# W1's units quantised first and p1 of the first two tiles put ahead of batch 3's values, in an attention and MXINT8 feed-forward kernel

## The chip, the cores and the metric

The kernel runs on one core of a Trainium2 chip. The metric is the device time of one execution in microseconds. Three runs of the kernel before took 282.99, 283.56 and 286.78 us, a median of 283.56.

## What is computed

For four batches of 512 tokens with 512 features and a context of 512 x 256:

```python
query = einsum('bnc,dc->bnd', ctx, Wq) + bq          # D = 128
key   = einsum('bnc,dc->bnd', ctx, Wk) + bk
attention = softmax(einsum('bnd,bmd->bnm', query, key))
x = x + einsum('bln,bmn->blm', layernorm(x), attention)

v = bf16(layernorm(x)); residual = v
h = bf16((v - mean(v)) * rsqrt(var(v) + 1e-5) * ln_w + ln_b)
h = bf16(mx_quant(h) @ mx_quant(W1).T + b1)          # 512 -> 2048
h = bf16(gelu_tanh(h))
h = bf16(mx_quant(h) @ mx_quant(W2).T + b2)          # 2048 -> 512
x = x + bf16(residual + h)
```

`mx_quant` rounds each block of 32 along the contraction to 8-bit integers with a shared power-of-two scale, from the block's largest absolute value.

## The kernel before

The program is written by hand, one instruction stream per engine, with semaphores between them. The order of each stream is the order of its code.

**Attention** goes batch by batch (`batch` on PE and ACT, `front` and `back` on VectorE, DVE). PE makes `energies` (L649), ACT the exponentials, DVE the low halves of p and x (`p_low`, `x_low`), SyncE (SP) transposes them by DMA (`xT` at L237, `pT` at L244), and PE makes `values` of the four 128-token tiles (L661, then L664, which adds x). ACT takes each out of PSUM in `x_plus` (L482) with its sum, takes the squares in `x1_square` (L490), POOL makes the row factors (`factors_x1`), and ACT writes the normalised rows v in `v_out` (L497) and their sums in `v_sums` (L505, L508). POOL's `factors_v` makes the factors of the second layer norm, and DVE applies it, a tile at a time, with `times_w` and `plus_b` (L961, L966), into `hq`. The block quantisation of a batch's `hq` is `h1_amax` to `h1_mult`, and gives `h1q`.

**Weights.** W1 and W2 come in four units each, [128, 2048] floats. There are two slots of the staging buffer `wst`, W1's and W2's. A unit goes through `w_amax` (L764), power, scale, inverse, `w_over` (L807), `w_clip` and `w_mult` (L817) on DVE, in steps placed in `front` and `back`, and then through a DMA transpose on SP (`w1_transpose`, `w2_transpose`). Unit u of W1 is finished in batch u's `back`, unit u of W2 in `front` of batch u+1, the last one after batch 3.

**Feed-forward**: 16 tiles of 128 tokens; tile i is (m, k) with i = 2m + k. For each one: SP transposes `h1q` (`h1_transpose`, L274, into `h1T`, which lies over cxT); PE makes p1 (`product1`: four bias matmuls L707 and 16 matmuls L712, into four PSUM banks); ACT takes the two halves out and applies GELU (`y_out`, L558 and L562, into `gs`, over phl); DVE quantises in `slot(m, k, tail)`; SP transposes the result (`h2_transpose`, L287); PE makes p2 (`product2`, 16 matmuls L722); ACT's `z_out` (L571), POOL's or DVE's two adds and SP's store end the tile. On PE p1 runs three tiles ahead of p2. Buffers are doubled. `ys` lies over the first slot of `wst`, `h2u` over `wquant`.

A DVE slot of tile i holds the clip of tile i-1, the block maximum (L764) of tile i, the last multiply (L871) of tile i-1, scale and inverse, and the multiply by the inverse (L861) of tile i. `tail` is other work put between them, as layer-norm steps of a coming batch. In `tail_parts(b)` parts 0 to 3 are the layer norm of batch b's four tiles, part 4 the block maximum and scales of h1, part 5 its three large operations.

PE's order before the steady loop is: values 0, p1(0), values 1, p1(1), values 2, values 3, p1(2), then steps.

Of the kernel before, what the change touches and what calls it, by code (L numbers as in the profile page):

```python
# [29 lines left out]
def xattn_ffn_kernel(nc, x, ctx_in, wq, bq, wk, bk, ln_w, ln_b, w1, b1, w2, b2, out):  # L30
# [25 lines left out]
    with ExitStack() as stack:  # L56
# [155 lines left out]

        @block.sync
        def _(sp):
# [37 lines left out]
            def w1_transpose(u):
                wait_alone(sp, w_step[W1], W_STEPS * (u + 1), sp_gate)
                sp.dma_start_transpose(
                    w1T[:, bass.ds(4 * u, 4), :, :].rearrange("p r k f -> p (r k) f"), wquant[:, W1, :])\
                    .then_inc(w1T_rdy, 16)

            def w2_transpose(u):
                wait_alone(sp, w_step[W2], W_STEPS * (u + 1), sp_gate)
                sp.dma_start_transpose(w2T[:, :, bass.ds(P * u, P)], wquant[:, W2, :]).then_inc(w2T_rdy, 16)  # L260
# [895 lines left out]
```

## Time and profile before

| | |
|---|---|
| runs, us | 282.99, 283.56, 286.78; median 283.56 |
| profiled execution, us | 283.25 |
| its span, us | 281.4 |
| busy of the span | DVE 89%, PE 81%, ACT 60%, POOL 25% |
| granted TensorE clock, mean | 0.927 of full speed |
| chain that ended last, by engine | DVE 45%, PE 25%, ACT 11%, DMA 8% |

The span runs from the first to the last instruction of the profiled execution, in microseconds from its start. A busy share is an average over the span. In the timelines a row is one instruction, or several of a kind merged (x4); the number in brackets is how long the engine stood idle before it, and who ended that. PE rows can overlap by a few tenths, since matmuls are pipelined and their ends are modelled.

### The profile page before, as it was taken

How to read it: one execution, taken by the hardware profiler on the slowest of the kernel's cores; microseconds unless marked ns; L12 is line 12 of the kernel's file. 1: busy time of each engine (PE TensorE's matmuls, PEld its weight loads, DVE VectorE, ACT ScalarE, POOL GpSimd, SP SyncE). 2: the span in 40 equal slices, each digit the busy share in tenths (PEclk: the TensorE clock that was granted, in tenths of full speed). 3: DMA queues.
4: the chain of work that ended last, by engine and by line, in shares of the span. 5: the costliest groups of instructions: out<-in, count | busy, mean ns of one | idle time of the engine just before them, and what ended most of it. 6: DMA issues, size and time to landing. Idle time of an engine off the chain costs nothing.

```text
span 281.4 us, 3244 instructions
## 1 busy us (share of the span) xinstructions
PE 228.7 (81%) x937; PEld 99.4 (35%) x946; DVE 249.2 (89%) x377; ACT 169.4 (60%) x287; POOL 69.0 (25%) x96
## 2 busy tenths in 40 slices
PE   7748739996998059651699969799999989999993
PEld 7314313443433024210244433344444434444431
DVE  2388999999988899999979999599999999877992
ACT  2337216628995447845987599966566554665610
POOL 1058100022004500053060050413333233333400
PEclk9985886999999759975899999999999999999999
DMA  4963999999997952939623045635355555555683
GB/s 157 378 250 89 227 279 201 297 238 194 263 257 190 221 91 38 222 59 194 124 52 62 0 93 70 119 62 123 88 122 129 130 130 131 130 130 114 139 178 130
DMA packets 103077, 42.92 MB, mean 152 GB/s; under 512 B 93844, under 2 KB 96152, under 8 KB 102552
## 3 DMA queue, kind: packets, MB, share of 16 engines
q1 hardware_dynamic: 100224, 35.93, 58.6%
q10 hardware_dynamic: 2360, 6.83, 7.7%
q8 instruction: 5, 0.08, 0.1%
q0 software_dynamic: 480, 0.02, 0.1%
q14 instruction: 8, 0.07, 0.1%
HBM read 15.48 MB, written 4.19 MB: 70 GB/s over the span
## 4 chain that ended last, share of the span: by engine, by line
DVE 45%; PE 25%; ACT 11%; DMA 8%; issue 5%; POOL 4%; SPq 2%; ACTq 0%; DVEq 0%; POOLq 0%
DVE amax L764 12%; PE ps L722 9%; PE ps L712 8%; PE ps L661 4%; DVE w_int L807 4%; DMA xhl<-pf 3%; DVE hq L966 3%; DVE stats L918 3%; DMA wst<-in_L_ffn_W 3%; DVE vw L961 3%; DVE pf L871 3%; DVE phl L942 2%; DVE wquant L861 2%; POOL rs L350 2%; DVE xhl L954 2%
## 5 line engine op out<-in xcount | busy, mean ns | idle before, releaser
L661 PE MATMUL ps<-pT,xT 128*128 128x512 f16 x192 | 49.7, 414 | 14.1 <-DMA pT<-phl 11.0
L722 PE MATMUL ps<-w2T,xhl 128*128 128x512 bf16 x247 | 56.5, 379 | 2.9 <-DMA xhl<-pf 2.4
L712 PE MATMUL ps<-w1T,cxT 128*128 128x512 bf16 x256 | 58.0, 380 | 0.0
L558 ACT ACTIVATE wst<-ps 128x1024 bf16<-128x1024 f32 x32 | 32.3, 1019 | 27.9 <-PE ps L712 27.9
L764 DVE TENSOR_REDUCE amax<-phl 128x64 f32<-128x2048 bf16 x16 | 36.5, 2280 | 6.9 <-ACT phl L562 6.9
L649 PE MATMUL ps<-qkT 128*128 128x512 f32 x32 | 19.5, 715 | 22.7 <-ACT pf L457 18.8
L661 PEld LDWEIGHTS ps<-pT,xT 128*128 128x128 f16 x192 | 19.9, 106 | 48.0 <-issue 31.8
L722 PEld LDWEIGHTS ps<-w2T,xhl 128*128 128x128 bf16 x256 | 24.6, 98 | 33.2 <-DMA xhl<-pf 4.2
L712 PEld LDWEIGHTS ps<-w1T,cxT 128*128 128x128 bf16 x256 | 23.7, 98 | 32.6 <-issue 6.2
L562 ACT ACTIVATE phl<-wst 128x2048 bf16<-128x2048 bf16 x16 | 30.6, 1910 | 1.3
L423 POOL TENSOR_TENSOR wst<-wst,vs 128x512 bf16<-128x512 bf16 x12 | 14.8, 1233 | 55.5 <-DVE wquant L866 55.5
L764 DVE TENSOR_REDUCE amax<-wst 128x64 f32<-128x2048 f32 x8 | 18.2, 2270 | 6.1 <-DMA wst<-in_L_ffn_W 6.1
L457 ACT ACTIVATE pf<-ps,nmax 128x512 f32<-128x512 f32 x16 | 10.9, 681 | 19.8 <-DVE nmax L928 19.7
L571 ACT ACTIVATE wst<-ps 128x512 bf16<-128x512 f32 x16 | 9.5, 595 | 16.2 <-PE ps L722 15.8
L861 DVE TENSOR_TENSOR wquant<-phl,mxi 128x2048 int16<-128x2048 bf16 x15 | 18.3, 1223 | 0.3
L641 PE MATMUL ps<-cxT,wqkT 128*128 128x512 f32 x32 | 16.5, 663 | 2.5 <-ACT cxT L447 2.5
L807 DVE TENSOR_TENSOR w_int<-wst,mxi 128x2048 int16<-128x2048 f32 x8 | 18.3, 2285 | 0.0
L871 DVE TENSOR_TENSOR pf<-wquant,mxs 128x2048 bf16<-128x2048 int16 x15 | 18.2, 1216 | 0.0
L649 PEld LDWEIGHTS ps<-qkT 128*128 128x128 f32 x32 | 5.9, 212 | 32.3 <-ACT pf L457 21.8
L355 POOL TENSOR_SCALAR rs<-mv 128x4 f32<-128x4 f32 x4 | 0.9, 227 | 65.6 <-DVE mv L923 65.6
L664 PE MATMUL ps<-xs,ident_x 128*128 128x512 f32 x32 | 16.3, 592 | 0.0
L482 ACT ACTIVATE xs<-ps 128x512 f32<-128x512 f32 x16 | 9.4, 586 | 9.7 <-PE ps L664 9.7
(79 smaller groups left out, 357.4 us busy)
## 6 DMA issues: line engine op xcount, KB each, us to landing
wst<-in_L_ffn_W ACTq DMA_DIRECT2D x6, 1024.0 KB, 6.1
xs<-in_x SPq DMA_DIRECT2D x4, 1024.0 KB, 8.4
out_x<-wst SPq DMA_DIRECT2D x16, 256.0 KB, 2.8
cx<-in_ctx SPq DMA_DIRECT2D x4, 512.0 KB, 5.8
wst<-in_L_ffn_W SPq DMA_DIRECT2D x2, 1024.0 KB, 10.3
xhl<-pf SPq DMA_TRANSPOSE x17, 4.3
xT<-xhl SPq DMA_TRANSPOSE x16, 4.6
pT<-phl SPq DMA_TRANSPOSE x16, 3.3
```

Of the source, the lines that this page charges most:

```text
L558: act.activation(ys[:, k, 1024 * g:1024 * g + 1024], ps_y[:, 2 * g:2 * g + 2, :], ACT.Copy)\
L562: act.activation(gs[:, k, :], ys[:, k, :], ACT.Gelu_apprx_tanh).then_inc(g_rdy, 1)
L641: last = pe.matmul(ps_qk[:, a, :], wqkT[:, a, c, :], cxT[:, c, :], start=(c == 0), stop=(c == CT - 1))
L649: pe.matmul(ps_e[:, t % 2, :], qkT[:, 0, P * t:P * t + P], qkT[:, 1, :], start=True, stop=True).then_inc(e_ps, 1)
L661: pe.matmul(ps_pv[:, t % 2, :], xT[:, t, NT * a + n, :], pT[:, :, NT * c + n, :], start=(s == 0), stop=False)
L664: pe.matmul(ps_pv[:, t % 2, :], ident_x[:, :], xs[:, LT * b + t, :], start=False, stop=True).then_inc(pv_ps, 1)
L712: last = pe.matmul(ps_y[:, c, :], h1T[:, k, t, :], w1T[:, 4 * c:4 * c + 4, t, :], start=False, stop=(t == KT - 1))
L722: last = pe.matmul(ps_z[:, k, :], h2T[:, k, t, :], w2T[:, t, :], start=False, stop=(t == FT - 1))
L764: dve.tensor_reduce(amax[:, a, :], by_block, AX_X, ALU.max, apply_absolute_value=True)\
L807: dve.tensor_tensor(blocks(w_int[:, :]), blocks(wst[:, a, :]), inverse, ALU.mult)\
L861: dve.tensor_tensor(pairs(h2u[:, k, :]), pairs(gs[:, k, :]), per_block(mxi[:, k, :, :]), ALU.mult).then_inc(h2_step[k], 1)
L871: dve.tensor_tensor(pairs(h2q[:, k, :]), pairs(h2u[:, k, :]), per_block(mxs[:, k, :, :]), ALU.mult).then_inc(h2_step[k], 1)
```

## The change

Weights: the two slots of `wst` are named EVEN and ODD and hold units of both matrices in a new order, given by the table UNITS. EVEN holds W1's units 0, 2, 3 and W2's 2; ODD holds W1's 1 and W2's 0, 1, 3. W1's last unit is so transposed in batch 2. SP's loop over batches 2 and 3 is written out.

First products: SP transposes `h1q` of tiles 0 and 1 ahead of batch 3's last pT. PE makes p1(0) and p1(1) ahead of batch 3's four values. ACT's `y_out` is split into `y_evict` and `gelu`; y(0) and y(1) are evicted among the `v_sums` of batch 2, and their GELUs come behind these.

Layer norms: DVE does batch 2's in the slots of tiles 1 to 4 and batch 3's in those of tiles 5 to 8. ACT's `x1_square` and `v_sums` of batch 3 are spread between evictions, and POOL's `factors_v(3)` comes after tile 0's adds.

```diff
-        W1, W2, H1 = range(3)
+        EVEN, ODD, H1 = range(3)
+        UNITS = (("w1", 0), ("w1", 2), ("w1", 3), ("w2", 2)), (("w1", 1), ("w2", 0), ("w2", 1), ("w2", 3))
...
+        def load_unit(eng, slot, u):
+            kind, n = UNITS[slot][u]
+            if kind == "w1":
+                return eng.dma_start(wst[:, slot, :].rearrange("p (r k) -> p r k", r=4), w1_t[n])
+            return eng.dma_start(wst[:, slot, :], w2_t[n])
...
                 for t in range(NT):
+                    if b == B - 1 and t == NT - 1:
+                        sp.wait_ge(h1_step, H_STEPS)
+                        sp.wait_ge(qk_ps, 2 * B)
+                        h1_transpose(0, 0)
+                        h1_transpose(0, 1)
                     wait_alone(sp, p_lo, b * NT + (t + 1), sp_gate)
...
-                w1_transpose(b)
+                if b > 0:
+                    transpose_unit(ODD, b - 1).then_inc(oddT_rdy, 16)
+                transpose_unit(EVEN, b).then_inc(evenT_rdy, 16)
...
-            with sp.Fori(2, B) as b:
-                front(b)
+            front(2)
...
-            sp.wait_ge(h1_step, H_STEPS)
-            sp.wait_ge(qk_ps, 2 * B)
-            h1_transpose(0, 0)
-            h1_transpose(0, 1)
-            w2_transpose(B - 1)
+            front(B - 1)
+            transpose_unit(ODD, B - 1).then_inc(oddT_rdy, 16)
...
-            factors_v(B - 1)
...
             for i in range(T - ON_DVE):
+                if i == 1:
+                    factors_v(B - 1)
                 add_residual(i)
                 add_x(i)
...
             for t in range(LT):
                 v_out(B - 2, t)
+            act.wait_ge(w_step[EVEN], W_STEPS * (B - 1) + 5)
+            y_evict(0, 0)
             v_sums(B - 2, 0)
             v_sums(B - 2, 1)
+            y_evict(0, 1)
             v_sums(B - 2, 2)
             v_sums(B - 2, 3)
             for t in range(NT):
                 act.wait_ge(pT_rdy[t], 16 * B)
-            for k in range(2):
-                x_plus(B - 1, k)
-                y_out(0, k)
-            x_plus(B - 1, 2)
-            x_plus(B - 1, 3)
-            for t in range(LT):
-                x1_square(B - 1, t)
+            gelu(0, 0)
+            x_plus(B - 1, 0)
+            gelu(0, 1)
+            for t in range(1, LT):
+                x_plus(B - 1, t)
+            x1_square(B - 1, 0)
+            x1_square(B - 1, 1)
             y_out(1, 0)
+            x1_square(B - 1, 2)
+            x1_square(B - 1, 3)
+            y_out(1, 1)
             for t in range(LT):
                 v_out(B - 1, t)
-            step(0, 0)
-            for t in range(LT):
-                v_sums(B - 1, t)
-            step(0, 1)
-            with act.Fori(1, T // 2 - 2) as m:
+            z_out(0, 0)
+            y_out(2, 0)
+            v_sums(B - 1, 0)
+            z_out(0, 1)
+            v_sums(B - 1, 1)
+            y_out(2, 1)
+            v_sums(B - 1, 2)
+            v_sums(B - 1, 3)
+            z_out(1, 0)
+            step(1, 1)
+            with act.Fori(2, T // 2 - 2) as m:
...
-            values(B - 1, 0)
...
-            pe.wait_ge(w1T_rdy, 16 * B)
+            pe.wait_ge(evenT_rdy, 16 * 3)
+            pe.wait_ge(oddT_rdy, 16)
+            pe.wait_ge(qk_sb, 2 * B)
+            product1(0, 0)
+            product1(0, 1)
             pe.wait_ge(p_exp, T)
-            for k in range(2):
-                if k > 0:
-                    values(B - 1, k)
-                product1(0, k)
-            values(B - 1, 2)
-            values(B - 1, 3)
+            for t in range(LT):
+                values(B - 1, t)
             product1(1, 0)
...
-            parts = tail_parts(B - 2)
-            for part in parts[:LT]:
-                for part_step in part:
-                    part_step()
-            dve.wait_ge(w1T_rdy, 16 * B)
-            slot(0, 0, parts[LT], True)
-            dve.wait_ge(w2T_rdy, 16 * B)
-            slot(0, 1, parts[LT + 1])
-            slot(1, 0, [])
-            parts = tail_parts(B - 1)
-            parts = [[], parts[0], parts[1] + parts[2]] + parts[3:]
-            for i in range(3, 3 + len(parts)):
-                slot(i // 2, i % 2, parts[i - 3])
+            p2, p3 = tail_parts(B - 2), tail_parts(B - 1)
+            dve.wait_ge(evenT_rdy, 16 * B)
+            slot(0, 0, [], True)
+            dve.wait_ge(oddT_rdy, 16 * B)
+            slot(0, 1, p2[0] + p2[1])
+            slot(1, 0, p2[2] + p2[3])
+            slot(1, 1, p2[LT])
+            slot(2, 0, p2[LT + 1])
+            slot(2, 1, p3[0])
+            slot(3, 0, p3[1] + p3[2])
+            slot(3, 1, p3[3] + p3[LT])
+            slot(4, 0, p3[LT + 1])
```

The names W1, W2, `ld_w1`, `w1T_rdy`, `load_w1` and so on become EVEN, ODD, `ld_even`, `evenT_rdy`, `load_even` throughout.

**PE, around the first products.** L661 and L664 are values, L707 and L712 are p1 (in the change L686, L689, L732, L737). Before, from the values of batch 3's first tile:

```order
L661 MATMUL ps<-pT,xT 128x512 x12
L664 MATMUL ps<-xs,ident_x 128x512
L707 MATMUL ps<-b1row,ones 128x512 x4
L712 MATMUL ps<-w1T,cxT 128x512 x16
L661 MATMUL ps<-pT,xT 128x512 x12
L664 MATMUL ps<-xs,ident_x 128x512
L707 MATMUL ps<-b1row,ones 128x512 x4
L712 MATMUL ps<-w1T,cxT 128x512 x16
L661 MATMUL ps<-pT,xT 128x512 x12
L664 MATMUL ps<-xs,ident_x 128x512
L661 MATMUL ps<-pT,xT 128x512 x12
L664 MATMUL ps<-xs,ident_x 128x512
```

and in the change, from the same place:

```order
L732 MATMUL ps<-b1row,ones 128x512 x4
L737 MATMUL ps<-w1T,cxT 128x512 x16
L732 MATMUL ps<-b1row,ones 128x512 x4
L737 MATMUL ps<-w1T,cxT 128x512 x16
L686 MATMUL ps<-pT,xT 128x512 x12
L689 MATMUL ps<-xs,ident_x 128x512
L686 MATMUL ps<-pT,xT 128x512 x12
L689 MATMUL ps<-xs,ident_x 128x512
L686 MATMUL ps<-pT,xT 128x512 x12
L689 MATMUL ps<-xs,ident_x 128x512
L686 MATMUL ps<-pT,xT 128x512 x12
L689 MATMUL ps<-xs,ident_x 128x512
```

Both p1 went ahead of the first values.

**ACT, from the end of batch 2's v_sums to the second GELU.** A pair of `squares` and `vs,sums<-vs` is one v_sums, `wst<-ps` x2 the eviction of a y, `phl<-wst` a GELU, `xs,sums<-ps` an x_plus. Before:

```order
L505 ACTIVATE squares,sums<-vs 128x512
L508 ACTIVATE vs,sums<-vs 128x512
L482 ACTIVATE xs,sums<-ps 128x512
L558 ACTIVATE wst<-ps 128x1024 x2
L562 ACT_TABLE_LOAD
L562 ACTIVATE phl<-wst 128x2048
L482 ACTIVATE xs,sums<-ps 128x512
L558 ACTIVATE wst<-ps 128x1024 x2
L562 ACTIVATE phl<-wst 128x2048
```

and in the change:

```order
L565 ACTIVATE wst<-ps 128x1024 x2
L512 ACTIVATE squares,sums<-vs 128x512
L515 ACTIVATE vs,sums<-vs 128x512
L512 ACTIVATE squares,sums<-vs 128x512
L515 ACTIVATE vs,sums<-vs 128x512
L572 ACT_TABLE_LOAD
L572 ACTIVATE phl<-wst 128x2048
L489 ACTIVATE xs,sums<-ps 128x512
L572 ACTIVATE phl<-wst 128x2048
```

The eviction of y(1) stands ahead of the last two v_sums, that of y(0) two v_sums further ahead, right behind v_out. The first x_plus went behind the first GELU.

**DVE, from the last weight unit to tile 1's maximum.** `w_int` and `wquant<-w_int` are the last unit, a pair of `vw` and `hq<-vw` is the layer norm of one tile, `amax<-phl` a tile's block maximum. Before, with the first of four layer-norm pairs:

```order
L807 TENSOR_TENSOR w_int<-wst,mxi 128x2048
L812 TENSOR_SCALAR w_int<-w_int 128x2048
L817 TENSOR_TENSOR wquant<-w_int,mxs 128x2048
L961 SCALAR_TENSOR_TENSOR vw<-vs,mean,lnw 128x512
L966 SCALAR_TENSOR_TENSOR hq<-vw,rs,lnb 128x512
```

and in the change:

```order
L831 TENSOR_TENSOR w_int<-wst,mxi 128x2048
L836 TENSOR_SCALAR w_int<-w_int 128x2048
L841 TENSOR_TENSOR wquant<-w_int,mxs 128x2048
L788 TENSOR_REDUCE amax<-phl 128x64
L796 TENSOR_SCALAR pow<-amax 128x64
L802 TENSOR_SCALAR mxs<-pow 128x128
L807 TENSOR_SCALAR mxi<-mxs 128x128
L885 TENSOR_TENSOR wquant<-phl,mxi 128x2048
L890 TENSOR_SCALAR wquant<-wquant 128x2048
L788 TENSOR_REDUCE amax<-phl 128x64
```

Nothing is left between the last unit and tile 0's maximum; the four pairs stand in the slots of tiles 1 and 2.

## Rows read from the trace of the kernel before

**Rows 1.** Page, part 1: busy us, share of the span, instructions.

```profile
PE 228.7 (81%) x937; PEld 99.4 (35%) x946; DVE 249.2 (89%) x377; ACT 169.4 (60%) x287; POOL 69.0 (25%) x96
```

**Rows 2.** DVE timeline, 144 to 227: start us, us, engine line op out<-in, [idle before].

```profile
146.45 0.75 DVE L961 SCALAR_TENSOR_TENSOR vw<-vs,mean,lnw 128x512 f32<-128x512 bf16 x1 [1.55 <-POOL rs L350]
...
152.25 2.28 DVE L764 TENSOR_REDUCE amax<-phl 128x64 f32<-128x2048 bf16 x1
...
168.08 2.28 DVE L764 TENSOR_REDUCE amax<-phl 128x64 f32<-128x2048 bf16 x1
...
173.99 2.28 DVE L764 TENSOR_REDUCE amax<-phl 128x64 f32<-128x2048 bf16 x1
...
182.82 2.29 DVE L764 TENSOR_REDUCE amax<-phl 128x64 f32<-128x2048 bf16 x1 [2.84 <-ACT phl L562]
...
189.94 2.28 DVE L764 TENSOR_REDUCE amax<-phl 128x64 f32<-128x2048 bf16 x1
...
198.53 2.28 DVE L764 TENSOR_REDUCE amax<-phl 128x64 f32<-128x2048 bf16 x1
...
222.99 2.28 DVE L764 TENSOR_REDUCE amax<-phl 128x64 f32<-128x2048 bf16 x1
...
225.58 1.21 DVE L871 TENSOR_TENSOR pf<-wquant,mxs 128x2048 bf16<-128x2048 int16 x1
```

**Rows 3.** PE timeline, 132 to 250.

```profile
132.47 4.29 PE L661 MATMUL ps<-pT,xT 128*128 128x512 f16 x12 [9.24 <-DMA pT<-phl]
...
139.79 0.40 PE L707 MATMUL ps<-b1row,ones 3*128 3x512 bf16 x4 [2.17 <-DMA cxT<-h1q]
140.12 3.63 PE L712 MATMUL ps<-w1T,cxT 128*128 128x512 bf16 x16
...
150.92 2.75 PE L661 MATMUL ps<-pT,xT 128*128 128x512 f16 x12
...
154.37 2.75 PE L661 MATMUL ps<-pT,xT 128*128 128x512 f16 x12
...
168.14 3.40 PE L722 MATMUL ps<-w2T,xhl 128*128 128x512 bf16 x15
...
231.38 3.63 PE L722 MATMUL ps<-w2T,xhl 128*128 128x512 bf16 x16 [0.96 <-DMA xhl<-pf]
...
246.48 3.62 PE L722 MATMUL ps<-w2T,xhl 128*128 128x512 bf16 x16
```

**Rows 4.** Windows, PE's wait before batch 3's values; 0.63 is PE's granted clock.

```profile
123.00:132.50 9.50, 0.26 (x2) 0.06 (x2) 9.39 (x15) 3.62 (x10) 5.79 (x9) 0.63 0.87 158
```

**Rows 5.** ACT timeline, 132 to 170.

```profile
132.64 2.93 ACT L497 ACTIVATE vs<-xs,off,rs 128x512 bf16<-128x512 f32 x4 [3.00 <-POOL off L370]
135.47 0.61 ACT L505 ACTIVATE squares<-vs 128x512 bf16<-128x512 bf16 x1
...
140.94 0.58 ACT L482 ACTIVATE xs<-ps 128x512 f32<-128x512 f32 x1
...
142.06 1.02 ACT L558 ACTIVATE wst<-ps 128x1024 bf16<-128x1024 f32 x1 [0.46 <-PE ps L712]
...
144.83 1.28 ACT L562 ACT_TABLE_LOAD   x1
146.12 1.91 ACT L562 ACTIVATE phl<-wst 128x2048 bf16<-128x2048 bf16 x1
...
158.02 0.60 ACT L482 ACTIVATE xs<-ps 128x512 f32<-128x512 f32 x1 [2.76 <-PE ps L664]
...
161.89 1.91 ACT L558 ACTIVATE wst<-ps 128x1024 bf16<-128x1024 f32 x2
...
166.40 2.93 ACT L497 ACTIVATE vs<-xs,off,rs 128x512 bf16<-128x512 f32 x4 [0.66 <-POOL off L370]
```

**Rows 6.** SP's queue, 124 to 140: issue start, us over all.

```profile
124.76 5.36 SPq L244 DMA_TRANSPOSE pT<-phl  x4
...
137.00 2.76 SPq L274 DMA_TRANSPOSE cxT<-h1q  x2
```

More of the change, by code:

```diff
@@ L247, in front, with transpose_unit @@
                     load_x(later)
-                if not isinstance(b, int) or b > 0:
-                    w2_transpose(b - 1)
-                w1_transpose(b)
[L252 to L260, printed above, removed]
+                if b > 0:
+                    transpose_unit(ODD, b - 1).then_inc(oddT_rdy, 16)
+                transpose_unit(EVEN, b).then_inc(evenT_rdy, 16)
+            def transpose_unit(slot, u):
+                kind, n = UNITS[slot][u]
+                wait_alone(sp, w_step[slot], W_STEPS * (u + 1), sp_gate)
+                if kind == "w1":
+                    return sp.dma_start_transpose(
+                        w1T[:, 4 * n:4 * n + 4, :, :].rearrange("p r k f -> p (r k) f"), wquant[:, slot, :])
+                return sp.dma_start_transpose(w2T[:, :, P * n:P * n + P], wquant[:, slot, :])
             load_ctx(1)
@@ L523, in batch @@
                     if t == 2 and b is not None:
-                        load_w2(front)
+                        load_odd(front)
                     if v is not None and t > 0:
@@ L531, in batch @@
                 if not isinstance(front, int) or front + 1 < B:
-                    load_w1(front + 1)
+                    load_even(front + 1)
                 if b is not None:
@@ L559, in y_out, with gelu @@
                        .then_inc(y_sb, 1)
+            def gelu(m, k):
+                i = 2 * m + k
                 act.wait_ge(y_sb, 2 * i + 2)
@@ L562, in y_out @@
                 act.activation(gs[:, k, :], ys[:, k, :], ACT.Gelu_apprx_tanh).then_inc(g_rdy, 1)
+            def y_out(m, k):
+                y_evict(m, k)
+                gelu(m, k)
             def z_out(m, k):
@@ L571, in z_out, with step @@
                 act.activation(zs[:, k, :], ps_z[:, k, :], ACT.Copy).then_inc(z_sb, 1)
+            def step(m, k):
+                if not isinstance(m, int) or 2 * m + k + 3 < T:
+                    y_out(*tile(m, k, 3))
+                z_out(m, k)
             for t in range(LT):
                 v_out(B - 2, t)
+            act.wait_ge(w_step[EVEN], W_STEPS * (B - 1) + 5)
+            y_evict(0, 0)
             v_sums(B - 2, 0)
             v_sums(B - 2, 1)
+            y_evict(0, 1)
             v_sums(B - 2, 2)
@@ L814, in w_mult @@
             def w_mult(a, u):
-                wait(dve, (w1T_rdy, w2T_rdy)[a], 16 * u)
+                wait(dve, (evenT_rdy, oddT_rdy)[a], 16 * u)
                 dve.wait_ge(w_step[a], W_STEPS * u + 6)
@@ L1047, in back @@
                         plus_b(tail, t)
-                w_clip(W1, w1)
-                w_mult(W1, w1)
+                w_clip(EVEN, w1)
+                w_mult(EVEN, w1)
             def tail_parts(b):
@@ L1060, in _ @@
             split3(b2_step, b2f, b2p)
-            w_amax(W1, 0)
-            w_power(W1, 0)
-            w_scale(W1, 0)
-            w_inverse(W1, 0)
+            w_amax(EVEN, 0)
+            w_power(EVEN, 0)
+            w_scale(EVEN, 0)
+            w_inverse(EVEN, 0)
             x_stats(0)
```

63 lines of the change are left out of this document (30 added, 33 removed).

## The prediction, made before the changed kernel ran

> **What bounds the kernel now.** I read the page's busy shares first: VectorE (DVE) 89%, TensorE (PE) 81% [rows 1]. An average over stages with different limits decides nothing, so I took the timelines of DVE, PE, ScalarE (ACT) and SyncE (SP) from the last batch of attention to the feed-forward tiles. Three things are to be seen.
>
> First, DVE works without a gap until the last weight unit is done. It then waits 1.55 us (until 146.45, so from 144.90) for the row factors of batch 2's layer norm, does that layer norm, and starts tile 0's block maximum at 152.25 [rows 2]. From there it goes from slot to slot, one slot per tile and one block maximum at the start of each. Its only other wait before tile 9 is 2.84 us, on ACT's GELU of tile 4 [rows 2]. DVE is thus idle 1.55 + 2.84 = 4.39 us between 144.90 and tile 9's maximum at 222.99.
>
> Second, PE's second product of tile 8 starts at 231.38, after a wait of 0.96 us for the transposed values [rows 3]. These come from DVE's multiply at 225.58 in slot 9 [rows 2]. That start stands 231.38 - 222.99 = 8.39 us behind the maximum of tile 9. After it every DVE slot is shorter than PE's 7.55 us a tile, (246.48 - 231.38) / 2 (a slot with nothing added takes 173.99 - 168.08 = 5.91 us [rows 2, 3]), and PE sets the end. So the end moves one for one with the later of two things: DVE's arrival at tile 9, and PE's own work before tile 8's second product.
>
> Third, before the feed-forward PE stands idle 9.24 us (from about 123.2), then 2.17 us more, then makes p1 of tiles 0 and 1 between the values; two sets of values without a gap are 154.37 - 150.92 = 3.45 us apart [rows 3]. The granted clock of 123.0 to 132.5 is 0.63 on average [rows 4], a mix of 2.4 and 1.2 GHz. The twelve matmuls after the wait take 4.29 us where the same twelve take 2.75 later [rows 3]. A start after that idle therefore costs about 1.5 us.
>
> **The slots of the weights.** The same eight units are loaded, quantised and transposed, by the same DVE forms. Only which matrix a slot holds changes. The SP loop becomes straight code, without its branches. I cost both at nothing. Their cover is DVE's gapless work: without it the loop could give or take at most about one issue of SP, 1.34 us [rows 6], since it runs through twice.
>
> **SP's order.** The four pT transposes of batch 3 are issued from 124.76 in 5.36 us, 1.34 each [rows 6]. In the change h1T of tiles 0 and 1 go in ahead of the fourth, at about 128.8, 1.34 us each. The fourth pT goes at about 131.5 instead of 128.8. Its readers, the values of batch 3, are now behind p1 on PE and start past 142, so this is hidden. Odd unit 2 is transposed at about 132.8, and DVE wants that slot back for unit 3 about 143: covered by some 10 us. If that cover went, DVE's arrival would move with it.
>
> **PE and ACT up to the first GELU.** This is the term that counts.
> - h1T(0) lands about 2.8 us after its issue (137.00 to 139.79 [rows 3, 6]): PE starts p1(0) at about 131.7. At full clock p1 takes 140.12 + 3.63 - 139.79 = 3.96 us. With 1.5 more for the clock it ends at about 137.2, its first half at 131.7 + 2.27 + 1.5 = 135.5 (139.79 to the eviction at 142.06 [rows 3, 5]).
> - ACT ends its four v_out at 132.64 + 2.93 = 135.57 [rows 5]. It evicts the halves of y(0) at 135.6 and 137.3, 1.02 each: done 138.3. PE's p1(1) waits for that and runs 138.4 to 142.4.
> - Two of four v_sums, which take 140.94 - 135.47 = 5.47 together, 2.74 for two [rows 5]: 141.1. Halves of y(1) at 141.1 and 142.4: done 143.4. Two more v_sums: 146.1.
> - Table load and GELU(0), 1.28 and 1.91 [rows 5]: **149.3**. Before, GELU(0) ended at 148.03, but DVE had layer-norm work until 152.25. Now it has none and waits from 144.90 to 149.3: 4.4 us of idle in place of 1.55.
>
> The table load stands directly in front of the GELU: 144.83 and 146.12 [rows 5], 1.29 us from start to start. The Trainium skill (ScalarE: Activation LUTs, What ACT_TABLE_LOAD costs) puts about 1.38 us of drain on top of each switch. By that rule the GELU would end 1.4 us later and the total below would be +2.4; the row shows no such gap, so the row is used.
>
> **The second wait.** ACT now does x_plus(0), then GELU(1), then x_plus(1). So PE makes the values of tile 2 from 150.0 (3.45 each), those of tile 3 to 156.9, and p1(2) to 160.8. The fourth pT has long landed by then. ACT, from x_plus(3) at 157.0: in the old order the step from 158.02 to 161.89 held x_plus, POOL's mean and four squares [rows 5]. With two squares (0.71 each) in place of four it is 2.45: 159.45. Second half of y(2) out at 161.8, GELU(2) at 163.7. DVE: slot 0 without its tail takes 4.8 us (5.91 less the 1.2 us multiply, which slot 0 has not), slot 1 now holds two tiles of layer norm, as slot 5 did (198.53 - 189.94 = 8.59 [rows 2]). So it is ready for tile 2's maximum at 149.35 + 4.8 + 8.59 = 162.75 and waits **0.95**.
>
> The later tiles have cover. Two squares (165.1), y(3) out (167.1), GELU(3) 169.0; DVE comes for it at 163.8 + 8.59 = 172.4. POOL's factors for v_out took 4.5 us behind the squares (161.89 to 166.40), so v_out of batch 3 ends at 165.1 + 4.5 + 2.93 = 172.5, z(0) at 173.1, y(4) is out at 175.0 and GELU(4) ends at 177.0; DVE comes at 172.4 + 5.91 or later. So the 2.84 us wait goes. PE's second product of tile 0 starts at about 165.9 instead of 168.14, since p1(3) starts when y(2) is out at 161.8 and takes 4.1 with its bias. By slot 3 it waits for DVE's results on every tile.
>
> **The layer norms moved.** Four pairs of operations of batch 2 go from ahead of slot 0 into slots 1 and 2, 5.8 us (146.45 to 152.25). The block work of h1 goes from slots 0 and 1 into 3 and 4, and batch 3's loses its free slot. All of it is still done before tile 9: DVE's sum of work between 144.90 and 222.99 is unchanged, which is why its idle time alone decides. Batch 3's factors on POOL now stand between tiles 0 and 1 of the residual adds. Their sums end on ACT at about 186.9 (from 177.0: a v_sums 1.4, z(1) 0.6, a v_sums 1.4, y(5) and its GELU 3.8, two v_sums 2.7), and batch 2's factors took 146.45 - 140.94 = 5.5 us behind theirs [rows 2, 5]: 192.4. DVE asks at about 193.3: nothing, with 1 us to spare.
>
> **Sum.** 4.40 + 0.95 - 4.39 = +0.96 us on DVE's way to tile 9, and so on the end. The profiled execution took 283.25 us (span 281.4), 0.31 below the median 283.56. So 284.2 on its scale, **284.5** as a median. Bounds of the term: GELU(0) can't end before 135.57 + 3.82 + 5.47 + 3.19 = 148.05 (four halves, four v_sums, load and GELU in one row), total -0.3. At the other end it ends at 155.5 (second rival), total +7.2. I take 149.3, since each wait in it is read from a neighbouring row.
>
> **Rivals.**
> 1. PE is the bound: its lead of 168.14 - 165.9 = 2.2 us reaches the end. For it: the chain behind tile 8 is PE's, and the front of the change is PE work. Against: PE's wait of 0.96 on DVE's output, and the slots' sum. The time is 283.56 - 2.2 = 281.3. At most all 4.39 us of DVE's idle goes, 279.2. Chance 0.20.
> 2. The clock stays down, the case that is slower. PE starts p1(0) after 8.5 us of idle, and p1(0) and p1(1) are parted by waits for ACT. If both run wholly at 1.2 GHz, p1(0) ends at 139.6 and is out at 140.6, p1(1) runs to 148.6 and is out at 149.6, two v_sums 152.3, GELU(0) 155.5. That is 6.2 later and +7.2 in all: 290.8. It decides from the point where p1(0)'s second half is still at half clock. Against: twelve matmuls were enough in the old order, after a longer idle, and a 2.17 us gap behind them cost nothing [rows 3]. The Trainium skill (TensorE: Matmul & The Clock Gate, Part 1) has idle gaps between bursts throttling the clock again each time; the 2.17 us gap here did not. Chance 0.07.
> 3. The change doesn't do what it says: the layer norm moved to slot 5 finds no factors, since they stand on POOL behind tile 0's adds and on ACT behind y(5), and DVE stops there. Price 1 to 2 us on top of the forecast, 286. Chance 0.10.
>
> **How the numbers follow.** Forecast 0.63, with its own range 283.2 to 286.0 (GELU(0) from 148.05 to 150.8). The range of 281.0 to 287.0 takes in most of the first rival and the third, and leaves out the second and the first's far end. Two per cent (5.7 us) is about what a measurement of this kernel tells from no change. The first rival can't reach that, since only 4.39 us of idle are there to win: faster 0.03 for what I have not seen. Slower 0.06, nearly all the second rival. Within 0.91.
>
> **What would show it.** Right: DVE idle of about 4.4 us before tile 0's maximum, about 1 before tile 2's, none at tile 4; p1(0) from about 131.7 and its first matmuls slow; PE's second product of tile 0 about 2 us sooner and of tile 8 not sooner, with PE waiting for DMA at most tiles from 2 to 8. Wrong: tile 0's maximum before 148.5, or tile 9's before 222, or a DVE wait on POOL in slot 5.

## The result, and the profile after

| | before | changed |
|---|---|---|
| median of 18 runs each, us | 283.79 | 285.44 |
| lowest and highest | 281.44, 287.64 | 283.21, 286.68 |
| profiled execution, us | 283.25 | 285.30 |
| its span, us | 281.4 | 283.5 |

The ratio of the changed kernel to the one before is 1.0069, with a 95% interval of 1.0042 to 1.0095: slower by 1.2 to 2.7 us, well inside two per cent. The forecast was 284.5 us, +0.96. The sign was right. The size was about half of what came, and the profile shows where the other half arose. Some executions of each kernel come out 1 to 2% longer than its fastest; the ratios leave them out, the medians don't, and the profiled executions of "v_sums(2) first" and of the first "GELU(0) first" below are of that kind.

The page's busy shares. DVE is 1.0 us busier than in [rows 1]. PE's 2.0 us more is mostly nine matmul records that the trace before lacks (x937 for x946), about 0.2 us each:

```profile
PE 230.7 (81%) x946; PEld 99.3 (35%) x946; DVE 250.2 (88%) x377; ACT 169.1 (60%) x287; POOL 66.1 (23%) x96
```

DVE's timeline, the rows that answer to [rows 2] (last weight multiply, then block maxima of tiles 0, 1, 2, 3, 4, 5, 6 and 9):

```profile
143.28 1.23 DVE L841 TENSOR_TENSOR wquant<-w_int,mxs 128x2048 bf16<-128x2048 int16 x1
149.32 2.29 DVE L788 TENSOR_REDUCE amax<-phl 128x64 f32<-128x2048 bf16 x1 [4.82 <-ACT phl L572]
...
154.31 2.28 DVE L788 TENSOR_REDUCE amax<-phl 128x64 f32<-128x2048 bf16 x1
...
163.92 2.29 DVE L788 TENSOR_REDUCE amax<-phl 128x64 f32<-128x2048 bf16 x1 [1.09 <-ACT phl L572]
...
172.36 2.28 DVE L788 TENSOR_REDUCE amax<-phl 128x64 f32<-128x2048 bf16 x1
...
180.69 2.28 DVE L788 TENSOR_REDUCE amax<-phl 128x64 f32<-128x2048 bf16 x1
...
189.41 2.28 DVE L788 TENSOR_REDUCE amax<-phl 128x64 f32<-128x2048 bf16 x1
...
197.68 2.28 DVE L788 TENSOR_REDUCE amax<-phl 128x64 f32<-128x2048 bf16 x1
...
225.06 2.28 DVE L788 TENSOR_REDUCE amax<-phl 128x64 f32<-128x2048 bf16 x1
```

Tile 9's maximum is 2.07 us later than the 222.99 of [rows 2], and the span is 2.1 longer. In its terms: the weights are done 0.40 earlier (144.50 for 144.90), idle time is 4.82 + 1.09 = 5.91 in place of 4.39 (+1.52), and the time DVE is not waiting is 80.56 - 5.91 = 74.65 in place of 78.09 - 4.39 = 73.70 (+0.95). The last was forecast as unchanged. It lies in the slot of tile 5, 197.68 - 189.41 = 8.27 us with one tile of layer norm, where the slot of tile 4 before took 189.94 - 182.82 = 7.12 with the same work [rows 2].

DVE in that slot, and then POOL at the same time (both timelines, same columns):

```profile
191.72 0.46 DVE L796 TENSOR_SCALAR pow<-amax 128x64 uint32<-128x64 uint32 x1
192.10 1.21 DVE L895 TENSOR_TENSOR pf<-wquant,mxs 128x2048 bf16<-128x2048 int16 x1
193.24 1.64 DVE L985 SCALAR_TENSOR_TENSOR vw<-vs,mean,lnw 128x512 f32<-128x512 bf16 x1
```

```profile
187.23 0.49 POOL L382 TENSOR_SCALAR mean<-sums 128x4 f32<-128x4 f32 x1 [3.92 <-ACT vs L515]
...
189.97 1.04 POOL L356 TENSOR_TENSOR rs<-rs,half 128x4 f32<-128x4 f32 x1
190.97 1.16 POOL L428 TENSOR_TENSOR wst<-wst,vs 128x512 bf16<-128x512 bf16 x1
192.21 2.12 POOL L434 TENSOR_TENSOR wst<-xs,wst 128x512 f32<-128x512 f32 x1
```

Batch 3's factors run from 187.23 to 191.01. So the adds of tile 1 begin 1.6 us behind the block maximum of 189.41. In the kernel before they began 0.23 us behind one (190.17 and 189.94). The second stands from 192.21 to 194.33 beside DVE's two-input operations: it takes 2.12 us, and the layer-norm operation 1.64 where its neighbours take 0.75. The ends fit two engines taking turns. POOL starts 0.11 us behind DVE's `pf` and ends 1.02 us behind that operation's end (193.31); `vw` starts while POOL holds on and ends 0.55 behind POOL's end. The Trainium skill (SBUF — State Buffer, SBUF: two separate sides) states such a rule: a DVE operation with two SBUF inputs and a GpSimd operation that reads SBUF exclude each other, whoever starts first holds the port pair, and "the other fully blocks". The trace agrees. It agrees also with what the rule leaves free: a maximum, with one input, beside the same adds costs neither anything (2.28 and 1.16, below). I had not weighed that rule.

PE, the rows that answer to [rows 3], and its granted clock by stretches (window, its length, PE busy, clock, DMA share, GB/s):

```profile
130.99 0.62 PE L732 MATMUL ps<-b1row,ones 3*128 3x512 bf16 x4 [8.13 <-DMA cxT<-h1q]
131.54 5.51 PE L737 MATMUL ps<-w1T,cxT 128*128 128x512 bf16 x16
138.26 0.40 PE L732 MATMUL ps<-b1row,ones 3*128 3x512 bf16 x4 [1.21 <-ACT wst L565]
138.59 3.63 PE L737 MATMUL ps<-w1T,cxT 128*128 128x512 bf16 x16
...
166.07 3.62 PE L747 MATMUL ps<-w2T,xhl 128*128 128x512 bf16 x16
...
233.43 3.63 PE L747 MATMUL ps<-w2T,xhl 128*128 128x512 bf16 x16 [0.97 <-DMA xhl<-pf]
```

```profile
131.00:135.00 4.00, 4.00 (x13) 0.50 0.89 168
135.00:136.00 1.00, 1.00 (x5) 0.81 1.12 196
136.00:137.00 1.00, 1.00 (x5) 1.00 1.12 213
```

Sixteen matmuls behind the 8.13 us wait take 5.51 for 3.63, at 1.2 GHz up to about 135. The second product of tile 0 is 2.07 us sooner than in [rows 3], that of tile 8 2.05 later: PE's lead is used up in waits.

ACT, the rows that answer to [rows 5]:

```profile
135.23 1.02 ACT L565 ACTIVATE wst<-ps 128x1024 bf16<-128x1024 f32 x1
137.09 1.02 ACT L565 ACTIVATE wst<-ps 128x1024 bf16<-128x1024 f32 x1 [0.83 <-PE ps L737]
...
142.25 1.02 ACT L565 ACTIVATE wst<-ps 128x1024 bf16<-128x1024 f32 x1 [0.50 <-PE ps L737]
...
146.02 1.28 ACT L572 ACT_TABLE_LOAD   x1
147.31 1.91 ACT L572 ACTIVATE phl<-wst 128x2048 bf16<-128x2048 bf16 x1
```

GELU(0) ends at 149.22. From the end of `v_out` (135.18) to the end of GELU(0) ACT has 14.04 us, and waits for PE in them 0.83 and 0.50 us. The rest is both evictions, four `v_sums` and the GELU: what DVE waits for is mainly ACT's order.

### The profile page after: what moved, and what is told of

It is laid out like the page before. It is cut to its first block, busy times and chain, and to the rows that moved or that the text cites. A ratio compares the mean times of both kernels' runs of the same rounds, so it can differ in the third digit from the quotient of the medians.

```text
span 283.5 us, 3197 instructions
## 1 busy us (share of the span) xinstructions
PE 230.7 (81%) x946; PEld 99.3 (35%) x946; DVE 250.2 (88%) x377; ACT 169.1 (60%) x287; POOL 66.1 (23%) x96
## 4 chain that ended last, share of the span: by engine, by line
DVE 48%; PE 26%; ACT 8%; DMA 8%; issue 5%; SPq 3%; POOL 2%; ACTq 0%; DVEq 0%; POOLq 0%
DVE amax L788 13%; PE ps L737 9%; PE ps L747 9%; DVE w_int L831 4%; PE ps L686 4%; DVE pf L895 3%; DMA xhl<-pf 3%; DVE stats L942 3%; DVE wquant L885 3%; DMA wst<-in_L_ffn_W 3%; DVE vw L985 3%; DVE hq L990 2%; DVE phl L966 2%; SPq L257 2%; DVE wquant L890 2%
## 5 line engine op out<-in xcount | busy, mean ns | idle before, releaser
L747 PE MATMUL ps<-w2T,xhl 128*128 128x512 bf16 x256 | 58.0, 379 | 6.2 <-DMA xhl<-pf 6.2
L737 PE MATMUL ps<-w1T,cxT 128*128 128x512 bf16 x256 | 59.9, 388 | 0.0
L686 PE MATMUL ps<-pT,xT 128*128 128x512 f16 x192 | 48.4, 406 | 5.6 <-ACT xs L489 4.5
L737 PEld LDWEIGHTS ps<-w1T,cxT 128*128 128x128 bf16 x256 | 24.2, 100 | 34.2 <-issue 8.9
L686 PEld LDWEIGHTS ps<-pT,xT 128*128 128x128 f16 x192 | 19.5, 103 | 38.8 <-issue 22.1
L732 PE MATMUL ps<-b1row,ones 3*128 3x512 bf16 x64 | 9.2, 395 | 9.3 <-DMA cxT<-h1q 8.1
L689 PE MATMUL ps<-xs,ident_x 128*128 128x512 f32 x32 | 16.3, 592 | 0.0
```

What stands on the lines that cost most here:

```text
L686: pe.matmul(ps_pv[:, t % 2, :], xT[:, t, NT * a + n, :], pT[:, :, NT * c + n, :], start=(s == 0), stop=False)
L689: pe.matmul(ps_pv[:, t % 2, :], ident_x[:, :], xs[:, LT * b + t, :], start=False, stop=True).then_inc(pv_ps, 1)
L737: last = pe.matmul(ps_y[:, c, :], h1T[:, k, t, :], w1T[:, 4 * c:4 * c + 4, t, :], start=False, stop=(t == KT - 1))
L747: last = pe.matmul(ps_z[:, k, :], h2T[:, k, t, :], w2T[:, t, :], start=False, stop=(t == FT - 1))
```

## Experiments

"Way" is the time from the start of DVE's last weight multiply (143.67 before, 143.28 after) to tile 9's maximum. It takes out the stages ahead: between profiled executions that last multiply starts anywhere from 141.34 to 144.90. It does not take out when ACT gets to GELU(0), so the way from tile 0's maximum to tile 9's is given too where that matters. Each ratio is to executions of the kernel before taken together with it (medians 283.37 to 283.88 us). The changed kernel ran 18 times, "LN2 back in front" 4, "the same again" and "changed, factors behind" 6, "the same, factors behind" 12, the others 10.

| kernel | median, us | ratio, interval | way, us |
|---|---|---|---|
| before | 283.79 | 1 | 79.32 |
| changed | 285.44 | 1.0069, 1.0042 to 1.0095 | 81.78 |
| units only | 281.61 | 0.9914, 0.9866 to 0.9961 | 77.78 |
| GELU(0) first | 280.39 | 0.9870, 0.9831 to 0.9910 | 77.64 |
| the same again | 280.71 | 0.9886, 0.9841 to 0.9932 | 77.88 |
| the same, factors behind | 281.45 | 0.9851, 0.9805 to 0.9897 | 78.24 |
| v_sums(3) early | 284.21 | 0.9998, 0.9951 to 1.0045 | 79.66 |
| v_sums(2) first | 284.01 | 1.0014, 0.9975 to 1.0054 | 80.71 |
| warm PE, 26 | 286.42 | 1.0080, 1.0038 to 1.0122 | 82.07 |
| warm PE, 36 | 286.08 | 1.0089, 1.0046 to 1.0132 | 82.34 |
| changed, factors behind | 286.71 | 1.0106, 1.0057 to 1.0154 | 82.03 |
| PE late | 286.50 | 1.0107, 1.0076 to 1.0137 | 82.37 |
| LN2 back in front | 288.45 | 1.0151, 1.0071 to 1.0232 | 84.63 |

The order by way is nearly the order by ratio.

**Batch 2's layer norm back ahead of slot 0**, all else as in the change:

```diff
+            for part in p2[:LT]: ...   # the four tiles
             dve.wait_ge(evenT_rdy, 16 * B)
-            slot(0, 0, [], True)
...
-            slot(0, 1, p2[0] + p2[1])
-            slot(1, 0, p2[2] + p2[3])
-            slot(1, 1, p2[LT])
-            slot(2, 0, p2[LT + 1])
+            slot(0, 0, p2[LT], True)
...
+            slot(0, 1, p2[LT + 1])
+            slot(1, 0, [])
+            slot(1, 1, [])
+            slot(2, 0, [])
```

> The changed kernel with batch 2's layer norm back ahead of slot 0 on DVE, its h1 block work back in slots 0 and 1, slots 2 to 4 without added work. Theory (DVE's idle time before tile 9 decides): POOL's factors of batch 2 end at about 148.4, so DVE waits there from 144.5, 3.9 us, and then no more for GELU(0) or GELU(2): 3.9 us of idle in place of 5.9. Tile 9's maximum at about 223.1 instead of 225.06, the end 2.0 us sooner than in the changed kernel, about level with before (ratio to before 0.998 to 1.003). Rival (PE's own chain decides): PE's order is untouched, so the end stays within 0.5 us of the changed kernel. Rival (the added cost is only POOL's contention in slot 5): also no change, since slot 5 is untouched.

It was far worse: 1.0151 of before, where 0.998 to 1.003 was expected. DVE's waits and what followed the last:

```profile
148.33 0.75 DVE L985 SCALAR_TENSOR_TENSOR vw<-vs,mean,lnw 128x512 f32<-128x512 bf16 x1 [3.77 <-POOL rs L356]
...
189.42 2.29 DVE L788 TENSOR_REDUCE amax<-phl 128x64 f32<-128x2048 bf16 x1 [1.47 <-ACT phl L572]
...
195.20 1.64 DVE L985 SCALAR_TENSOR_TENSOR vw<-vs,mean,lnw 128x512 f32<-128x512 bf16 x1 [2.13 <-POOL rs L356]
196.76 1.17 DVE L802 TENSOR_SCALAR mxs<-pow 128x128 bf16<-128x128 f32 x1
```

Layer norm first waits for the factors, since ACT now makes the v_sums behind two evictions: 3.77 for the 1.55 of before. And empty slots 2 to 4 bring DVE to tile 5 before its GELU and before batch 3's factors. That is 7.37 us of idle against 4.39 before and 5.91 in the changed kernel, with a collision in slot 5 (11.17 us for 8.27, 2.13 of it the wait). Behind ACT's new order the layer norm stands better behind slot 0. The forecast had the first wait right (3.9) and missed the two in slot 5.

**Batch 3's v_sums ahead of y(5)** on ACT:

```diff
             v_sums(B - 1, 1)
-            y_out(2, 1)
             v_sums(B - 1, 2)
             v_sums(B - 1, 3)
+            y_out(2, 1)
```

> The changed kernel with ACT's last two v_sums of batch 3 ahead of y(5) instead of behind it. Theory (POOL's add of tile 1 fell out of tile 5's block maximum since the factors of batch 3 came late, and held up DVE's layer-norm operation, 1.64 us in place of 0.75): the factors end before 189, POOL's adds of tile 1 run beside tile 5's maximum at 189.4, the layer-norm operation in slot 5 takes 0.75 again, slot 5 is 7.1 us in place of 8.27, and the end comes about 1.0 us sooner than in the changed kernel. Rival (slot 5 is long for another reason): slot 5 stays at 8.3 and the end stays. GELU(5) comes about 2.5 us later, at 186.5, still ahead of DVE.

From tile 0's to tile 9's maximum it took 74.74 us, 75.74 in the changed kernel: 1.00 less, as expected. (Its way is 2.12 less, but 1.13 of that is a shorter wait before tile 0, 3.69 for 4.82, which stands ahead of the edit.) DVE in slot 5, then POOL:

```profile
189.80 2.28 DVE L788 TENSOR_REDUCE amax<-phl 128x64 f32<-128x2048 bf16 x1
...
193.53 0.74 DVE L985 SCALAR_TENSOR_TENSOR vw<-vs,mean,lnw 128x512 f32<-128x512 bf16 x1
```

```profile
190.03 1.16 POOL L428 TENSOR_TENSOR wst<-wst,vs 128x512 bf16<-128x512 bf16 x1
191.27 1.16 POOL L434 TENSOR_TENSOR wst<-xs,wst 128x512 f32<-128x512 f32 x1
```

The factors are done just in time, at 190.06. The adds run beside the maximum, the second 0.35 us beyond it, and neither they nor the layer-norm operation are stretched. Slot 5 took 7.28 us for 8.27, with its tile of layer norm still in it. The median is 1.2 us lower, by the ratios 2.0. This shows the second half of the loss.

**PE kept busy ahead of p1(0)**, so that it might start at 2.4 GHz; and the same with 36 small matmuls:

```diff
             pe.wait_ge(c_ones, 1)
+            pe.wait_ge(x1_rdy, (B - 1) * LT)
+            keep_busy(26)
             pe.wait_ge(row_b1, 16 * 3 * LT)
```

> The changed kernel with 26 small matmuls on PE between batch 2's last values and p1(0), which fill its 8 us of idle; their result is not used. Theory (a start at 1.2 GHz costs p1(0) 1.6 to 2 us, and that reaches DVE through the evictions): p1(0)'s 16 matmuls take 3.6 us in place of 5.5, y(0) is out 1.3 to 1.7 us sooner, and GELU(0) and DVE's first maximum come 0.8 to 1.7 us sooner (ACT's own work is the limit at 148.0), the end as much. Rival (the clock does not come back through such matmuls, or the wait for them delays p1(0)): no gain, or up to 1 us later.

> As e3_warm with 36 small matmuls instead of 26. In e3 they ended 2.0 us ahead of p1(0), and the granted clock was 0.5 again when p1(0) began. Now they reach up to p1(0), at most 0.5 us past its data. Theory: the clock stays at 2.4 GHz, p1(0)'s 16 matmuls take 3.6 us in place of 5.5, y(0) is out 1.5 us sooner counted from p1(0)'s start, and DVE's first maximum 1.2 to 1.5 us sooner counted from there (18.3 us in the changed kernel, 17.8 in e3, about 17.0 here). Rival (small matmuls do not hold the clock): p1(0) takes 5 us or more, and nothing is gained.

PE with 26, then with 36:

```profile
121.77 6.04 PE L640 MATMUL ps<-ident 128*128 128x128 f32 x52 [0.87 <-ACT xs L489]
129.83 0.62 PE L732 MATMUL ps<-b1row,ones 3*128 3x512 bf16 x4 [2.02 <-DMA cxT<-h1q]
130.38 5.02 PE L737 MATMUL ps<-w1T,cxT 128*128 128x512 bf16 x16
```

```profile
123.34 8.28 PE L640 MATMUL ps<-ident 128*128 128x128 f32 x72 [1.60 <-ACT xs L489]
131.55 0.40 PE L732 MATMUL ps<-b1row,ones 3*128 3x512 bf16 x4
131.87 3.63 PE L737 MATMUL ps<-w1T,cxT 128*128 128x512 bf16 x16
137.72 0.40 PE L732 MATMUL ps<-b1row,ones 3*128 3x512 bf16 x4 [2.22 <-ACT wst L565]
138.05 5.31 PE L737 MATMUL ps<-w1T,cxT 128*128 128x512 bf16 x16
```

With 26 the clock is 1.00 up to the 2.02 us wait and half behind it. With 36 p1(0) runs at full clock, but then PE waits 2.22 us for ACT, and p1(1) is slow instead. From p1(0)'s start to tile 0's maximum it is 18.33 us in the changed kernel, 17.84 and 18.93 here, and neither kernel is faster than the changed one: the forecasts of 0.8 to 1.7 us and 1.2 to 1.5 us both missed. What a full clock in both products would give is not shown. It is at most the 0.83 and 0.50 us that ACT waited for PE in the changed kernel.

**PE late by seven small matmuls** ahead of tile 0's second product:

```diff
+                    pe.wait_ge(x1_rdy, B * LT)
+                    keep_busy(7)
                 product2(m, k)
```

> The changed kernel with 7 small matmuls (about 1.6 us) on PE ahead of tile 0's second product; their result is not used. Theory (DVE's arrival at tile 9 decides, PE has slack): tile 0's second product starts 1.6 us later, tile 8's at the same 233.4, and the end stays within 0.4 us. Rival (PE's own work before tile 8's second product decides): the end comes 1.6 us later, ratio to the changed kernel 1.006.

Tile 0's second product came 1.56 us later behind tile 0's maximum (18.31 for 16.75). From maximum 0 to 9 it took 76.30 us, 0.56 over the changed kernel, 0.54 of it in slot 5 (8.81): v_sums(3) ended later, and so did the factors and the adds. The median is 1.1 us higher, between the 0.4 of the theory and the 1.6 of the rival, and decides nothing. The trace does: tile 8's second product stood 8.37 us behind tile 9's maximum, as in the changed kernel. So PE is not the bound, and its lead buys nothing; it matters only through ACT and POOL.

**The weights' order and an earlier place for h1T on SP**, with PE, ACT and DVE in the order of before. SP transposes h1T of tiles 0 and 1 ahead of the last weight units, right behind batch 3's last pT; in the change they stand ahead of that pT:

```diff
 (the kernel before)
+        UNITS = (("w1", 0), ("w1", 2), ("w1", 3), ("w2", 2)), (("w1", 1), ("w2", 0), ("w2", 1), ("w2", 3))
+                if b == B - 1:          # ahead of w2's and w1's transposes
+                    h1_transpose(0, 0)
+                    h1_transpose(0, 1)
-            with sp.Fori(2, B) as b:
-                front(b)
+            front(2)
```

> The kernel before with one part of the change alone: the units of W1 and W2 in the slots in the new order, SP's loop written out, and h1T of tiles 0 and 1 transposed right behind batch 3's last pT. PE's, ACT's and DVE's orders of work are those of before. Theory: p1(0) starts when values 0 end, at about 137.6 instead of 139.8, but DVE still waits 1.5 us for batch 2's factors and then works through; only GELU(4) comes sooner, so its 2.84 us wait shrinks to about 1.4, and the end comes about 1.4 us sooner than before, ratio 0.995. Rival (PE's order decides): 2.2 us sooner, ratio 0.992. Rival (the new order of the units costs DVE or SP something in batches 1 to 3): slower than before, and DVE's last weight multiply later than 143.7 against its first maximum.

DVE, its only two waits:

```profile
145.94 0.75 DVE L979 SCALAR_TENSOR_TENSOR vw<-vs,mean,lnw 128x512 f32<-128x512 bf16 x1 [1.55 <-POOL rs L364]
...
180.77 2.29 DVE L782 TENSOR_REDUCE amax<-phl 128x64 f32<-128x2048 bf16 x1 [1.29 <-ACT phl L576]
```

The 1.55 stays, the 2.84 shrinks to 1.29, as expected, way -1.54. p1(0) starts at 137.19, without a wait for its transposes. This, nearly a part of the change, is a gain of 0.4 to 1.3% by itself. The reordering of PE, ACT and DVE more than gave it back. Which of its two edits brings the gain was not tested apart.

**All v_sums of batch 2 ahead of y(0)'s eviction**, with the layer norm in front and batch 3's v_sums early:

```diff
-            v_sums(B - 2, 0)
-            v_sums(B - 2, 1)
+            for t in range(LT):
+                v_sums(B - 2, t)
             y_evict(0, 1)
-            v_sums(B - 2, 2)
-            v_sums(B - 2, 3)
```

> As e1_ln2_back, and on ACT all four v_sums of batch 2 ahead of the eviction of y(1), and v_sums of batch 3 ahead of y(5). Theory (sum of DVE's waits before tile 9, and each of them set by ACT's order): the factors of batch 2 come at about 147.3 instead of 148.3, so the first wait is 2.8 us in place of 3.8; at tile 5, where e1 waited 1.47 us for GELU(5) and 2.13 for the factors, about 2.5 in all remain; tile 9's maximum 2 us sooner than in e1, the end as much, ratio to before about 1.005. Rival (PE's chain): the end as in e1, since PE's order is the same.

Its waits were 1.83 for the factors and 3.54 for GELU(5), 5.37 together, 2.00 less than with LN2 back in front. The first wait is nearly that of before. The second is the cover that is gone when slots 2 to 4 are empty: a wait moved, not removed.

**GELU(0) right behind y(0)'s eviction.** DVE takes slot 0 at once, and the layer norm in slot 1:

```diff
             y_evict(0, 0)
-            v_sums(B - 2, 0)
-            v_sums(B - 2, 1)
-            y_evict(0, 1)
-            v_sums(B - 2, 2)
-            v_sums(B - 2, 3)
...
             gelu(0, 0)
+            for t in range(LT):
+                v_sums(B - 2, t)
+            y_evict(0, 1)
+            gelu(0, 1)
...
-            for t in range(LT):
-                values(B - 1, t)
-            product1(1, 0)
+            values(B - 1, 0)
+            values(B - 1, 1)
+            product1(1, 0)
+            values(B - 1, 2)
+            values(B - 1, 3)
...
-            slot(0, 1, p2[0] + p2[1])
-            slot(1, 0, p2[2] + p2[3])
-            slot(1, 1, p2[LT])
-            slot(2, 0, p2[LT + 1])
+            for part in p2[:LT]: ...   # behind slot 0
+            slot(0, 1, p2[LT])
+            slot(1, 0, p2[LT + 1])
+            slot(1, 1, [])
+            slot(2, 0, [])
```

The v_sums of batch 3 stand ahead of y(5) too.

> The changed kernel with GELU(0) right behind the eviction of y(0), ahead of the v_sums of batch 2; DVE does slot 0 first and batch 2's layer norm between slots 0 and 1, its block work in slots 1 and 2; PE makes p1(2) between batch 3's values 1 and 2; v_sums of batch 3 ahead of y(5). Theory (DVE's idle time decides): GELU(0) ends at about 141.3, before DVE is done with the weights, so no wait at 144.5; the factors of batch 2 come before 149.3; a wait of about 1 us for GELU(5) remains. Tile 9's maximum at about 219.7, the end 2.9 us sooner than before and 5 sooner than in the changed kernel, ratio to before 0.990. Rival (PE decides): PE does the same work from the same start, so the end is within 1 us of the changed kernel.

> The variant with GELU(0) right behind y(0)'s eviction once more, beside the two others. It was 0.987 of before (0.983 to 0.991). If that stands, 0.985 to 0.99 again, 280.0 to 281.0 us; if the gain came with the front stage's run-to-run differences, 0.99 to 1.0.

It beats both kernels, twice. DVE in the second of these executions:

```profile
144.90 1.23 DVE L840 TENSOR_TENSOR wquant<-w_int,mxs 128x2048 bf16<-128x2048 int16 x1
146.04 2.28 DVE L787 TENSOR_REDUCE amax<-phl 128x64 f32<-128x2048 bf16 x1
...
152.13 0.75 DVE L984 SCALAR_TENSOR_TENSOR vw<-vs,mean,lnw 128x512 f32<-128x512 bf16 x1 [1.82 <-POOL rs L356]
...
190.96 1.65 DVE L984 SCALAR_TENSOR_TENSOR vw<-vs,mean,lnw 128x512 f32<-128x512 bf16 x1
```

The 4.82 before tile 0 is gone, one wait of 1.82 is left (1.55 in the first execution, none was expected there), and the collision in slot 5 (1.65 for 0.75) is still there. Against the changed kernel the way is 3.9 to 4.1 us shorter, and the idle time 4.1 to 4.4. The variant is several moves at once, not tested apart. Against the kernel before the way is 1.4 to 1.7 us shorter; the medians say 3.1 to 3.5 us. Part of what lies between is the choice of executions: the two profiled ones took 1.9 and 2.4 us more than their medians, that of the kernel before 0.5 less than its own. Where the faster executions gain, in the way or ahead of it, no profile shows.

**Batch 3's factors behind tile 1's adds**, in the changed kernel and in the last one:

```diff
-                if i == 1:
+                if i == 2:
                     factors_v(B - 1)
...
-            slot(2, 1, p3[0])
-            slot(3, 0, p3[1] + p3[2])
-            slot(3, 1, p3[3] + p3[LT])
+            slot(2, 1, [])
+            slot(3, 0, p3[0] + p3[1])
+            slot(3, 1, p3[2] + p3[3] + p3[LT])
```

> The changed kernel with one part altered: on POOL the factors of batch 3's second layer norm stand behind tile 1's two residual adds and no longer between tile 0's and tile 1's, and DVE applies that layer norm in the slots of tiles 6 and 7 (two tiles each, the block maximum of h1 behind them in slot 7) in place of 5, 6 and 7. DVE's work is the same. Theory (tile 1's adds pushed out of the block maximum by the factors run beside a layer-norm operation of DVE and stretch both): the adds of tile 1 start with the block maximum of tile 5, both take 1.16 us, every layer-norm operation takes 0.75 us, the factors follow and are done before DVE asks in slot 6. From tile 0's maximum to tile 9's it takes 74.7 us in place of 75.74, and the median is 0.8 to 1.2 us below the changed kernel's, 284.4, about 1.003 of before. Rival (slot 5 was long because it held a tile of layer norm, wherever that stands): the sum stays 75.7 us and the median 285.4. Second rival (the slot of 11.6 us at tile 7 starves PE): DVE's sum falls but PE's second product of tile 8 starts more than 8.5 us behind tile 9's maximum, and the median stays.

> The variant with GELU(0) right behind y(0)'s eviction (280.39 us, 0.987 of before), with batch 3's factors put behind tile 1's adds on POOL and that layer norm in slots 6 and 7. If the stretching of the adds and the layer-norm operation was worth about 1 us in it too (slot 5 took 8.0 us there where 7.1 were due, one operation 1.64 us against 0.75), the way from tile 0's maximum to tile 9's falls from 76.5 to about 75.6 and the median to about 279.5, 0.984 of before. If not, it stays at 280.4. If the long slot 7 starves PE, it is 281 or more.

In the changed kernel it took 75.85 us from maximum 0 to 9, where 74.7 was expected: nothing gained. POOL, DVE and PE:

```profile
197.81 1.15 POOL L428 TENSOR_TENSOR wst<-wst,vs 128x512 bf16<-128x512 bf16 x1
199.04 2.20 POOL L434 TENSOR_TENSOR wst<-xs,wst 128x512 f32<-128x512 f32 x1
```

```profile
200.14 1.65 DVE L985 SCALAR_TENSOR_TENSOR vw<-vs,mean,lnw 128x512 f32<-128x512 bf16 x1
```

```profile
225.94 4.98 PE L747 MATMUL ps<-w2T,xhl 128*128 128x512 bf16 x16 [3.91 <-DMA xhl<-pf]
```

The adds of tile 1 were clean (slot 5 took 6.07), but the factors now held up those of tile 2, and the same collision stood in slot 6, at the same price. That speaks for the order on POOL as its cause and against slot 5 itself, as does the slot 5 of 7.28 us above. Slots 5 to 7 took 6.07 + 9.34 + 11.63 = 27.04 us against 25.94 in the kernel with v_sums(3) early: 0.9 is the collision, and 0.2 that a tile of layer norm is not equally dear in each slot. It added 1.21 us to an empty slot before (7.12 for 5.91), and 1.55 to slot 7, which already held another tile and h1's block maximum (11.63 for 10.08). That the first fills pauses between short operations would explain it, but is not shown. The slot of 11.63 also let PE wait 3.91, and its next matmuls took 4.98 for 3.63; tile 8's second product stood 8.58 behind the maximum, 0.2 more than usual. In the other kernel the collision did go, but DVE then met GELU(6) 0.72 us early, and slots 5 to 7 took 27.29 against 26.67. Its ratio can't be told from that of the kernel without it, and its median, 281.45, missed the expected 279.5.

## Why the prediction was right, and where its size was not

- **What bounds the kernel**: right. Tile 8's second product stood 8.37 us behind tile 9's maximum (8.39 in the working), and the end moved as DVE did: 2.07, 2.05 and 2.1 us at the maximum, at PE and in the span.
- **Up to the first GELU**: right. p1(0) began at 130.99 (131.7) and ended at 137.05 (137.2), y(0) was out at 138.11 (138.3), y(1) at 143.27 (143.4), GELU(0) at 149.22 (149.3). The wait was 4.82 for 4.40, since DVE came 0.4 sooner. No drain stood at the table load: 146.02 to 147.31 is 1.29.
- **Second wait**: 1.09 for 0.95, and none at tile 4. The two waits and what went came to +1.52, less 0.40 from the front: +1.1 for +0.96.
- **The step that failed** is "DVE's sum of work ... is unchanged", with "nothing, with 1 us to spare" for batch 3's factors. They were in time for DVE's question (ready 191.0, asked 193.24). But I had asked only who waits for them, not who stands behind them on POOL: tile 1's adds, which must run under the block maximum. Pushed out from under it, they cost 0.95, shown by taking it away (v_sums(3) early, -1.00), by making it larger (PE late, +0.56), and by its moving to slot 6 with the factors.
- **Slots of the weights, SP's order, at nothing**: fair as a term of the change, since the front was 0.4 us sooner, less than it differs between executions. But nearly the same orders of units and of SP, with the old PE, ACT and DVE orders, are a gain of 0.9%, and that was not looked for.
- **Rival 1**, PE as bound, is out: PE's lead of 2.07 us came and brought nothing. **Rival 2**, the clock: p1(1) ran at full clock after its 1.21 us wait, as forecast. The case was nearer than it seemed: behind 2.02 and 2.22 us the clock fell in the two warm kernels, though not behind 2.24 us at the same place in "v_sums(3) early". The prediction's sentence on the Trainium skill leaves out that the Trainium skill (TensorE: Matmul & The Clock Gate, Part 1) speaks there of gaps beyond a certain length, so the 2.17 us gap is no case against it. **Rival 3** named the place, slot 5, and nearly the price, but with a wait of DVE on POOL that didn't come. The forecast case and a cost of rival 3's size were both there: 285.4 lies between their 284.5 and 286. That the time fell inside the stated range says nothing for the step that failed: the range had room for its 0.95 us.

## What to carry to other kernels

When a step is moved on a side engine, ask what is queued behind it there, and beside which instructions of the bound engine that will now run; an add hidden under a one-input reduction is free, the same add beside a two-input operation stops both. Feeding the matrix engine earlier is worth nothing where another engine sets the pace: the first product's way through ACT to DVE counts, and ACT should bring out what DVE can start on (here GELU(0)) before what it needs later. Test the parts of a bundled change alone; what was nearly one of them was a gain that the others gave back.
